# Batch normalisation of the mixer: channel statistics in the projection pass, scale, shift and rectifier in the tile copies of the next loop

## What is computed

```python
h = logmap0(proj(x, c), c)                       # rows scaled by a function of their norm
h = conv1d(transpose(h), w_qkv, pad=2)           # middle tap: 256 -> 768 channels
mean = jnp.mean(h, axis=(0, 2), keepdims=True)   # per channel, over all 3125 rows
var = jnp.var(h, axis=(0, 2), keepdims=True)
h = gamma * (h - mean) * rsqrt(var + 1e-5) + beta
h = relu(h)
# then: expmap0/proj, depthwise and grouped 1x1 convolutions, linear attention
# per row, a 512 -> 256 convolution with bias, and Moebius addition to x
```

## Time and profile before

| what | value |
|---|---|
| median of 3 runs | 6925.64 us (6922.27 to 6926.2) |
| profiled execution | 6930.48 us |
| its span, first to last instruction | 6928.6 us |
| TensorE, VectorE, ScalarE, GpSimd busy | 74%, 65%, 34%, 58% of the span |
| mean granted clock of TensorE | 0.862 of full speed |

### The profile page before, as it was taken

One profiled execution on the slowest core, in us unless ns is written; L12 is line 12 of the kernel. 1 busy time (PEld: TensorE's weight loads), 2 busy tenths in 40 slices (PEclk: granted clock), 3 DMA queues, 4 the chain that ended last, 5 costly groups with the idle time before them and its releaser, 6 DMA issues. The chain is left out here.

```text
span 6928.6 us, 101720 instructions
## 1 busy us (share of the span) xinstructions
PE 5120.9 (74%) x27238; PEld 3844.2 (55%) x27238; DVE 4531.2 (65%) x7921; ACT 2381.2 (34%) x6607; POOL 4031.3 (58%) x4040
## 2 busy tenths in 40 slices
PE   3445588888857888888677668989989886877723
PEld 1334455555545555555566457758768675766622
DVE  8467599999966999998692265474664745211157
ACT  3143155555532555555321322222222221222211
POOL 1566677777747777775007665556655652577720
PEclk9777799999978999998888889989999997888855
DMA  2000377777725777775200223324333242222101
GB/s 43 24 1 5 114 224 224 220 220 217 218 70 159 223 221 221 220 218 172 54 14 7 61 69 96 114 70 116 101 87 114 74 119 76 46 45 58 27 3 59
DMA packets 362044, 766.26 MB, mean 111 GB/s; under 512 B 133276, under 2 KB 189493, under 8 KB 360552
## 3 DMA queue, kind: packets, MB, share of 16 engines
q0 software_dynamic: 232848, 605.63, 32.1%
q1 hardware_dynamic: 128707, 154.57, 7.4%
HBM read 717.16 MB, written 42.74 MB: 110 GB/s over the span
## 5 line engine op out<-in xcount | busy, mean ns | idle before, releaser
L1809 POOL DMA_INDIRECT arena<-kv_rows,visit_src x1616 | 1647.8, 1020 | 571.8 <-issue 477.3
L2386 POOL DMA_INDIRECT arena<-piece_rows,visit_src x808 | 800.7, 991 | 613.6 <-issue 317.2
L2070 ACT CAST ps<-cat 125x265 bf16 x1616 | 619.6, 383 | 671.4 <-issue 383.0
L1962 PE MATMUL ps<-arena,w 125*128 x4848 | 785.2, 311 | 82.7 <-DVE stage_ht L1849 66.9
L1962 PEld LDWEIGHTS ps<-arena,w 125*128 125x128 bf16 x4848 | 513.1, 106 | 376.0 <-issue 205.1
L931 POOL DMA_INDIRECT sorted<-arena,cat x512 | 542.5, 1060 | 167.4 <-issue 157.7
L2816 POOL DMA_INDIRECT arena<-tab,visit_src x537 | 514.5, 958 | 185.6 <-issue 184.7
L2071 ACT COPY arena<-ps x1616 | 604.6, 374 | 0.3
L931 POOL DMA_INDIRECT by_low<-steer x400 | 387.3, 968 | 358.1 <-PEq L91 160.6
L855 PE MATMUL ps<-stage_ht,w 128*128 128x250 f32 (+1 forms) x2496 | 556.7, 379 | 20.7 <-DVE stage_ht L887 15.5
L2467 DVE TENSOR_TENSOR arena<-arena,ps 125x256 f32 x808 | 339.9, 421 | 317.0 <-PE ps L2448 242.3
(11 more groups left out here) (605 smaller groups left out, 9710.5 us busy)
## 6 DMA issues: line engine op xcount, KB each, us to landing
w<-rel SPq DMA_DIRECT2D x102, 500.0 KB
arena<-kv_rows,visit_src POOLq DMA_INDIRECT x1616, 4.6
arena<-rel SPq DMA_DIRECT2D x34, 512.0 KB
arena<-piece_rows,visit_src POOLq DMA_INDIRECT x808
kv_rows<-h SPq DMA_DIRECT2D x50, 250.0 KB
arena<-tab,visit_src POOLq DMA_INDIRECT x537
sorted<-arena,cat POOLq DMA_INDIRECT x512
w<-in_L_mix_W SPq DMA_DIRECT2D x8, 1024.0 KB
```

The lines of the kernel that those rows point to most:

```text
L1809: nc.gpsimd.indirect_dma_start(ring[k % RG][:, j, :], None, d.kv, bass.IndirectOffsetOnAxis(g.srcv[:, v:v + 1], 0)).then_inc(got[k % RG], 16)
L1962: ins = nc.tensor.matmul(psQ[:, j * D:(j + 1) * D], ohT[b % 4][:, e:e + EP], q[:, bass.ds(at[j], D)], start=(m == 0), stop=(m == 2))
L2070: nc.scalar.copy(flat[0:P, bass.ds(clean[j], WIDE)], zeros[:, 0:WIDE]).then_inc(s["zeroed"], 1)
L2386: nc.gpsimd.indirect_dma_start(self.rows[v % (self.RG * GG)], None, self.d.pieces, bass.IndirectOffsetOnAxis(g.srcv[:, v:v + 1], 0)).then_ ...
```

## The change

The channel statistics are taken in the projection pass: after the copies of pair i, VectorE runs six `bn_stats` over pair i - 1 in H3 (each gives count, mean and squared deviations for the even and the odd columns). In the normalisation block the sum, the squares and the in-place pass are gone; VectorE combines the 26 partial means and deviations of each channel group in eleven small steps, ScalarE takes the root, and scale and shift are made as before. The second loop's tile copy becomes six ACTIVATEs, one for each channel group, with the rectifier, shift and scale of the channel. The scatters are dealt out anew: 6 in place of 42 in the normalisation block, 214 in place of 190 in the second loop, and thereby 68 in place of 56 beside the first projection of the attention layer.

```diff
+    seen = g.view(12800, 6 * 6 * len(pairs)).rearrange("p (j i c) -> p j i c", j=6, c=6)
     with phase(nc, g, "staged", "turned", "fetched", "made", "kept", "kept_c") as (block, s):
...
+            def count(i):
+                t, n = pairs[i]
+                dve.wait_ge(s["kept"], i + 1)
+                dve.wait_ge(s["kept_c"], i + 1)
+                for j in range(6):
+                    nc.vector.bn_stats(seen[:, j, i, :], H3[:, j, t * P:(t + n) * P])
+
             fetch(0)
             for i, (t, n) in enumerate(pairs):
...
                 ins.then_inc(s["kept"], 1)
+                if i:
+                    count(i - 1)
+            count(len(pairs) - 1)
...
-        scatter.beside(42)(block, s)
+        scatter.beside(6)(block, s)
...
-            act.wait_ge(s["means"], 1)
-            for j in range(6):
-                ins = nc.scalar.activation(g.view(12800, N), H3[:, j, :], ACT.Square, bias=nmean[:, j:j + 1],
-                                           accum_out=var[:, j:j + 1])
-                ins.then_inc(s["squares"], 1)
-                act.wait_ge(s["squares"], j + 1)
+            act.wait_ge(s["spread"], 1)
             nc.scalar.activation(sc, var, ACT.Sqrt, bias=g.eps[:, :], scale=1.0 / N).then_inc(s["rooted"], 1)
-            act.wait_ge(s["ready"], 1)
-            for j in range(6):
-                ins = nc.scalar.activation(H3[:, j, :], H3[:, j, :], ACT.Relu, bias=sh[:, j:j + 1], scale=sc[:, j:j + 1])
-            ins.then_inc(s["done"], 1)
-            act.wait_ge(s["done"], 1)
...
-            step(V.tensor_reduce(mean, H3, AX, ALU.add))
-            step(V.tensor_scalar(mean, mean, 1.0 / N, None, ALU.mult))
-            V.tensor_scalar(nmean, mean, -1.0, None, ALU.mult).then_inc(s["means"], 1)
+            means, squares = G3[:, :, :, 1], G3[:, :, :, 2]
+
+            def weighted(out, of):
+                step(V.tensor_reduce(out, of[:, :, 0:groups - 2], AX, ALU.add))
+                step(V.scalar_tensor_tensor(out, of[:, :, groups - 2], even / P, out, ALU.mult, ALU.add))
+                step(V.scalar_tensor_tensor(out, of[:, :, groups - 1], odd / P, out, ALU.mult, ALU.add))
+
+            weighted(mean, means)
+            step(V.tensor_scalar(mean, mean, float(P) / N, None, ALU.mult))
+            step(V.tensor_tensor(off, means, mean.unsqueeze(2).to_broadcast([128, 6, groups]), ALU.subtract))
+            step(V.tensor_tensor(off, off, off, ALU.mult))
+            weighted(var, off)
+            step(V.tensor_reduce(part, squares, AX, ALU.add))
+            V.scalar_tensor_tensor(var, var, float(P), part, ALU.mult, ALU.add).then_inc(s["spread"], 1)
...
-            scatter.along(190, "out_ready", range(1, NT + 1))(block, s)
+            scatter.along(214, "out_ready", range(1, NT + 1))(block, s)
...
-                    nc.scalar.copy(hjT[u], H3[:, :, bass.ds(t * P, P)]).then_inc(s["taken"], 1)
+                    for j in range(6):
+                        ins = nc.scalar.activation(hjT[u][:, j, :], H3[:, j, bass.ds(t * P, P)], ACT.Relu, bias=sh[:, j:j + 1],
+                                                   scale=sc[:, j:j + 1])
+                    ins.then_inc(s["taken"], 1)
```

More of the change, by code:

```diff
@@ L1379, in _ @@
                 ins.then_inc(s["kept"], 1)
-    mean, nmean, var, sc, sh = (g.vec[:, 6 * k:6 * k + 6] for k in range(5))
+                if i:
+                    count(i - 1)
+            count(len(pairs) - 1)
+    mean, part, var, sc, sh = (g.vec[:, 6 * k:6 * k + 6] for k in range(5))
+    groups = 2 * len(pairs)
+    G3 = g.view(12800, 18 * groups).rearrange("p (j q c) -> p j q c", j=6, c=3)
+    off = g.view(13400, 6 * groups).rearrange("p (j q) -> p j q", j=6)
+    even, odd = float((P + 1) // 2), float(P // 2)
     gb, bb, dw = (g.vec[:, 6 * k:6 * k + 6] for k in range(5, 8))
@@ L1385, in mix @@
     brw = g.w1[0:P, MIX:MIX + D]
-    with phase(nc, g, "loaded", "zeroed", "placed", "step", "means", "squares", "rooted", "ready", "done") as (block, s):
-        scatter.beside(42)(block, s)
+    with phase(nc, g, "loaded", "zeroed", "placed", "step", "spread", "rooted") as (block, s):
+        scatter.beside(6)(block, s)
         @block.sync
@@ L1429, in _ @@
             step(V.tensor_tensor(sh, mean, sc, ALU.mult))
-            V.tensor_tensor(sh, bb, sh, ALU.subtract).then_inc(s["ready"], 1)
+            V.tensor_tensor(sh, bb, sh, ALU.subtract)
     FT = g.b2
```

## The result

The changed kernel took 6892.63 us (median of 5 runs, 6884.83 to 6899.87) beside 6924.4 us for the kernel before: ratio 0.9953, 95% interval 0.9939 to 0.9966 (24 to 42 us), **31.8 us faster**. The forecast was 6887.0, that is 38.6 less, and the range 6879 to 6899.

The account below looks back on a forecast made before the run. Blocks closed by all-engine barriers bound the kernel; in normalisation VectorE and ScalarE work one after the other. -48.7 + 0 + 1.6 + 2.0 + 6.5 = -38.6 us takes the median from 6925.64 to 6887.0 us, range 6879 to 6899.

Parts of the forecast that it names:

- Normalisation block: Long sum, squares and rectifier passes go; loads then set its length, first tile copy at 337.4 for 386.1: -48.7 us.
- Rival F: Normalisation block isn't shortened because its loads or scatters fill it; they need 10 us, not 50; no chance of its own.
- Statistics: Projection pass: 78 bn_stats, 2.0 us for six, fit VectorE's idling and end at 305 us under GpSimd's scatters: 0 us.
- Rival D: Projection pass: bn_stats slow GpSimd's scatters, which end the block, by 3 to 7 us, up to 6894; chance 0.08.
- Tile copy: Second loop: six ACTIVATEs take 2.4 us, 1.6 more than one COPY; 0 us a tile, +1.6 us at the head.
- Rival E: Second loop: the six ACTIVATEs lie on the chain, 1.6 us in each of 24 tiles, 6925.4 or 6943; chance 0.03.
- 24 scatters in the loop: Second loop: 8.6 scatters a tile fit; the last ends at 680.8 for 678.8 and GpSimd ends the loop: +2.0 us.
- wrong: a lag that grows with the scatters: Sign against the forecast: time from last scatter to next block, taken as 6.0 to 7.15 us after long runs, grows.
- Rival C: Second loop: GpSimd becomes its clock, at 1.40 us a scatter; priced at 6 us, 6893; chance 0.08.
- 12 scatters in the attention projection: Attention layer's first projection: last scatter ends 14.0 us later against 13.2 or 7.2 us of slack: +6.5 us.
- Rival B: Attention projection: GpSimd's end stays hidden, +0.8 us for +6.5, 6881.3; chance 0.10.

Follow-up runs that it names:

- e2: The kernel before the change, unedited, run again for a second profile: 6930.89 us; its one profiled execution took 6940.49 us.
- e1: The changed kernel, unedited, run again: 6894.49 us, ratio 0.9947 to the kernel before.
- e3: The changed kernel's statistics and tile copies with the old deal of scatters (42, 190, 56): 6930.83 us, ratio 1.0001 to the kernel before.
- e5: The changed kernel with each of a tile's six ACTIVATEs cut in two: 6896.59 us in one execution, beside 6928.28 for the kernel before.
- e6: The changed kernel with each of a tile's six ACTIVATEs cut in four: 6976.35 us in one execution, second loop 380.9 us.
- e7: The changed kernel with 226 scatters in the second loop and 56 beside the attention projection: 6888.64 us, ratio 0.9938 to the kernel before.
- e4: The kernel before, with its old statistics, normalisation and copies, but the new deal of scatters (6, 214, 68): 6940.4 us, ratio 1.0012.
- e9: The changed kernel with scatters 6, 220 (24 chunks, one earlier), 16 at the mixer's end, 66 in the attention projection, started early: 6882.86 us, ratio 0.9924.
- e8: The changed kernel with 7 scatters in normalisation, 213 in the loop one chunk earlier, and the attention projection's started at once: 6885.77 us, ratio 0.9934.

## Why the prediction was right

The forecast for the part up to the end of the attention projection was -38.6 us; the profiles of before and after give -38.4 (821.3 to 782.9). Its mechanism held in every block but for the lag behind the loop's scatters (below). The agreement to 0.2 us is luck: the terms missed by +1.0 (normalisation), -0.9 (loop) and +0.7 (attention projection), the blocks that the sum had at nothing by -0.5 together, and by the second profiles of both kernels (e2, e1) the same point comes 42.6 us earlier. By its steps:

- **Normalisation block, -48.7 forecast, -47.7 measured.** To the first tile copy it took 12.11 us and not 11.1. The load of the 1x1 weights landed 9.4 us after the block's start in place of the 8.2 that I read off a low DMA share: +1.3. VectorE's six scalings and four steps took 1.96 us for 2.2, and 0.72 us passed to the copy for 0.9: -0.4. Removing the long sums bared the loads, as the step said. Rival F was right to get no chance with 6 scatters; with 42 it is e3, the whole effect.
- **Statistics, 0 forecast, 0 measured.** 2.01 us for six bn_stats, end at 304.9 for 305, block 98.5 against 98.6 us. Rival D falls: the 70 scatters were busy 67.02 us, 67.23 before, 0.96 us each in both.
- **Tile copy, +1.6 at the head, 0 a tile.** Six ACTIVATEs took 2.40 us for 2.4. The head, from the first copy to VectorE's first work, grew by 1.07 us (6.92 to 7.99), less than forecast. From the first copy to VectorE's last result the loop took 297.3 us, 298.1 before, so 25 tiles didn't grow but gave 1.8 us: the longer tile of each pair fell from 11.8 to 11.6 us, for a reason that wasn't looked into. Rival E is excluded by e3's loop and its point of decision shown by e5 and e6. The Trainium skill, "ScalarE: Activation LUTs", section "What ACT_TABLE_LOAD costs", makes an estimated 424 ns of one ACTIVATE of half the columns and 398 ns of a quarter, before their overlap; the medians of e5 and e6 were 425 and 398, so its price holds down to 31 columns.
- **24 scatters in the loop, +2.0 forecast; the loop's +3.6 in all was +2.7.** Two errors hide in it, and that they partly cancel is luck. The last scatter ended 1.0 us later after the first copy, not 3.6; and the lag, which I took as fixed, grew from 7.15 to 8.8. The second is the sign that the prediction named as "wrong: a lag that grows with the scatters". It came true, at 1.6 us, and yet the lag isn't a matter of their count: behind 226 it was 1.6 us (e7). Rival C, GpSimd as the clock of every tile, falls: tiles got no longer; at 226 it does pass VectorE, at the end only.
- **12 scatters in the attention projection, +6.5 forecast, +7.2 measured.** The last scatter ended 89.9 us after the block's start for 76.4 (13.5 later, 14.0 forecast), and the slack of 7.2 us behind the landing was used up: GpSimd's closing step ends 0.2 us before the next block. Rival B (hidden) falls by that and by e7, which with 56 is back at 100.0. But not all of the 7.2 us is GpSimd's: SP was done with the writes of kv_rows 103.3 us after the block's start, 99.6 before, so that 3.7 us would have come without its close. Against the other profile of the kernel before, with 104.0 us, the growth is only 2 to 3.5 us: kv_rows' writes are late there, and the longer wait for them hides as much of the scatters. So +6.5 holds against a block that the writes end early and is too much against one that they end late.

**Between the sum and the medians.** The profile's whole difference was -45.6 us and that of the medians -31.8. The first has 6.5 us of edge attention, untouched code, at 1144.8 us, the lowest of 13 profiles (up to 1154.8). Such spread is as large as anything left open here; the three medians' differences, 31.8, 36.4 and 42.0, have a mean of 36.7.

## What to carry to other kernels

In a block where two engines' lists end within a few us of each other, cost the removal of either alone at nothing and look for the edit that moves both: alone e3 gave nothing and e4 cost 8 to 10 us, together they gained 32 to 42. Work moved off a bare block should go where an engine has idling behind which nothing waits: 78 bn_stats were free in a block that GpSimd ends, and the dearer tile copy in a loop whose tiles VectorE sets. The room is not that of the engine that does the work (ScalarE's 5.8 us a tile) but that of the ring it lies on, here TensorE's 1.3 to 2.1 us. After such a change read again which list ends each block: one chunk less at the loop's end took GpSimd's close off it and gave 5 us more, and an earlier start in the attention projection 3.

## What the runs showed of the hardware

**GpSimd's close behind its scatters.** Between the last scatter's end and the end of GpSimd's closing step (in the trace, its drain ahead of the barrier) lay, in all profiles, the attention projection aside, where GpSimd's loads come between:

| scatters in the block | place | us |
|---|---|---|
| 6, 7 | normalisation | 1.5 to 1.9 |
| 10 | norms of the mixer | 1.65 |
| 12 | layer norm | 1.7 |
| 16 | mixer's end (e9) | 5.69 |
| 20 | mixer's end | 6.9 to 8.1 |
| 42 | normalisation | 3.49 |
| 70 | projection pass | 5.78 |
| 190 | second loop | 6.92 |
| 213, 214 | second loop | 8.55 |
| 220 | second loop (e9) | 9.04 |
| 226 | second loop (e7) | 1.39 |

It repeats to a few hundredths for the same list, but for the mixer's end and the 6 of the normalisation block. It isn't the landing: the scatters' packets are through 1 to 2 us after the last one. It isn't the count either, with 8 us behind 20 and 1.4 behind 226. In e7 GpSimd paused 1.72 us ahead of its last three scatters, for no cause that the trace shows. What GpSimd does in this time stays open. The prediction took it as a cost of 6 to 7 us behind a long run, and e8 hid it; neither explains it.

**A neighbour without harm.** Eighteen bn_stats, with two copies between them, beside GpSimd's scatters left these at 0.96 us, where VectorE's products at the mixer's end made them 1.10.
